# Image 1's loads and weight preparation reordered, image 2's moments and x loads moved, in a two-image attention and motif kernel

## The reference

```
x = x + attention(_gn(x))     # layer 1
x = x + motif(_gn(x))         # layer 2
# attention: qkv = 1x1 conv(x, w_qkv) + b_qkv;  qkv = depthwise 3x3 conv(qkv, w_dw) + b_dw
#   q, k normalised over the pixels; attn = softmax(q k^T * temperature) per head: 4 heads of 24 channels
#   out = 1x1 conv(attn v, w_out) + b_out
# motif: per group of planes the squared distances of shifted patches, the nearest neighbour, then
#   floor(motif * motif_nn * count / Cg), added back over nine shifts
```

## Time and profile before

| | |
|---|---|
| median of 3 runs (lowest, highest) | 1575.14 us (1575.06, 1578.28) |
| profiled execution, its time | 1579.09 us |
| its span | 1577.1 us |
| TensorE, VectorE, ScalarE, GpSimd busy | 85, 73, 56, 43 % of the span |
| mean granted clock of TensorE | 0.934 |
| `prepare` | 0 to 41.2 us |
| attention of image 1, of image 2 begin | 41.2 us, 788.5 us |
| terms of image 1, of image 2 begin | 513.3 us, 1304.5 us |

### The profile page before, as it was taken

How to read it: one execution, slowest core, us unless ns; L and a number is a source line. 1 busy time by engine, 2 the same in 40 slices (tenths; PEclk the granted TensorE clock), 3 DMA queues, 4 the chain that set the end, 5 groups by cost and what they waited for, 6 DMA issues and landing times. The chain is left out here.

```text
span 1577.1 us, 33962 instructions
## 1 busy us (share of the span) xinstructions
PE 1338.1 (85%) x13569; PEld 1079.0 (68%) x13569; DVE 1144.1 (73%) x1903; ACT 879.2 (56%) x950; POOL 680.3 (43%) x680
## 2 busy tenths in 40 slices
PE   0799999996988699999767887889978986999996
PEld 0699887985987355555356777888968983555553
DVE  8577675468864699999645565663786856999995
ACT  1455563212541699999634444542215526999995
POOL 3698892452220335440057566752533303354400
PEclk9999999898999799999969898997989997999998
DMA  6366631792141546453236655423901415464432
GB/s 224 88 209 203 195 90 32 212 273 93 42 168 75 180 123 178 100 142 72 52 101 182 182 155 169 126 62 101 273 5 70 193 62 172 131 178 100 142 72 51
DMA packets 78850, 208.12 MB, mean 132 GB/s; under 512 B 15633, under 2 KB 19827, under 8 KB 76035
## 3 DMA queue, kind: packets, MB, share of 16 engines
q1 hardware_dynamic: 64228, 153.09, 31.5%
q0 software_dynamic: 7296, 40.08, 9.9%
q10 hardware_dynamic: 7168, 12.78, 3.0%
HBM read 89.39 MB, written 67.04 MB: 99 GB/s over the span
## 5 line engine op out<-in xcount | busy, mean ns | idle before, releaser
L1663 PE MATMUL acc<-rnd,ident 128*128 128x376 f32 x1152 | 391.6, 483 | 24.7 <-ACT rnd L1642 24.7
L886 PE MATMUL ps_a<-wa,xa 128*128 128x192 f16 x1536 | 305.3, 251 | 12.7 <-DVE y_s L615 12.5
L1663 PEld LDWEIGHTS acc<-rnd,ident 128*128 128x128 f32 x1152 | 216.5, 192 | 145.3 <-ACT rnd L1642 26.0
L886 PE MATMUL ps_a<-wb,xb 128*128 128x192 f16 x1536 | 303.7, 250 | 0.0
L1510 DVE TENSOR_TENSOR prod<-fc,near 128x1504 f32<-128x1504 f32 x144 | 247.3, 1717 | 33.1 <-DMA near<-f_planes,index 17.4
L1637 ACT ACTIVATE rnd_m<-prod,plus_round,scale 128x1504 f32<-128x1504 f32 x144 | 235.8, 1637 | 61.6 <-DVE prod L1510 51.0
L549 POOL TENSOR_TENSOR vt<-z 96x256 f32<-96x256 f32 x248 | 256.6, 1055 | 18.7 <-ACT z L790 18.6
L1611 DVE SCALAR_TENSOR_TENSOR over<-prod,scale,rnd 128x1504 bf16<-128x1504 f32 x144 | 255.5, 1777 | 0.0
L1555 POOL DMA_INDIRECT near<-f_planes,index x56 | 159.0, 2840 | 209.8 <-DVE prod L1510 201.8
L1642 ACT ACTIVATE rnd<-rnd_m,minus_round 128x1504 f32<-128x1504 f32 x144 | 223.2, 1550 | 4.8
L886 PEld LDWEIGHTS ps_a<-wa,xa 128*128 128x128 f16 x1536 | 154.1, 100 | 19.7 <-issue 18.2
(11 more groups left out here) (304 smaller groups left out, 2390.3 us busy)
## 6 DMA issues: line engine op xcount, KB each, us to landing
xb<-xa ACTq DMA_DIRECT2D x64, 195.0 KB, 2.7
f_planes<-img SPq DMA_DIRECT2D x8, 1536.0 KB, 14.0
fc<-f_planes SPq DMA_DIRECT2D x16, 768.0 KB, 5.5
out<-done_rows POOLq DMA_DIRECT2D x16, 768.0 KB, 8.2
v_a<-xa SPq DMA_DIRECT2D x40, 260.0 KB, 2.7
v_b<-xb SPq DMA_DIRECT2D x40, 260.0 KB, 3.2
xa<-v_a SPq DMA_DIRECT2D x40, 260.0 KB, 4.9
xb<-v_b SPq DMA_DIRECT2D x40, 260.0 KB, 5.5
```

The lines of the kernel that those rows point to most:

```text
L886: mm = lambda a, w, first, end: nc.tensor.matmul(out(i), a, w, start=first, stop=end)
L1663: nc.tensor.matmul(o(m), k["ident"][:, :], rnd[:, n % RNDS, BR * m:BR * m + BR, :], start=False, stop=False, skip_group_check=True)
```

## The change

- `prepare`: SP issues x first. The weights go through ScalarE's queue, w_dw no longer broadcast. TensorE folds: it transposes w_qkv and w_dw (six transposes), ScalarE and GpSimd scale identities into diagonals `diag_w`, and six float32 matmuls w_t x diagonals give the combined weights, which ScalarE rounds to `wqk_hi` and copies to `w_32`, and GpSimd splits to `wqk_lo`. Of the stacking DMAs four stay on SP and nine go to ScalarE's queue (`stack_rest`).
- VectorE in `prepare` has only the statistics and then the moments (`channel_moments`), which were in attention's block.
- VectorE's constants go into units 2 to 9 of image 1 (`constants`), the layout of `wv_u`, `wv_c` to ScalarE in units 4 to 15 (`lay_out`, three activations each, scaled by a column of taps).
- Image 2: its moments are computed at the start of image 1's `motif_terms`, and its x comes in four loads (`load_stretch`, units 0-1, 2-7, 8-19, 20-31).
- Small buffers of `motif_grams` now lie in `g_half`, and `padded` counts in one step more.

```diff
+def channel_moments(nc, dve, c, k, part, mom, mom_c, ps, ps_col, sems):
...
+    group_stats(nc, dve, c, k["stats"], k["dev"], part, ps, mom, sems["stat_ready"], sems["stat_summed"],
+                sems["stat_rooted"])
...
+            for q in range(NQ):
+                sp.dma_start(img[:, QROWS * q:QROWS * (q + 1), :], x[0][:, QROWS * q:QROWS * (q + 1), :]
+                             ).then_inc(x_in[q], 16)
...
+            sp.wait_ge(split, 6)
+            stack_weights(sp, wqk_hi, wqk_lo, k["wa"], k["wb"], stacked)
+            sp.wait_ge(moved, 16 * 18)
...
+            pool.wait_ge(zeroed, COMBINED)
+            nc.gpsimd.tensor_tensor(diag_w[:, 1], k["ident"][0:C, 0:C].unsqueeze(1).to_broadcast([C, 12, C]),
+                                    taps[:, 1, :].unsqueeze(2).to_broadcast([C, 12, C]), ALU.mult).then_inc(zeroed, 1)
...
+            for j in range(6):
+                h, g = divmod(j, 3)
+                at = (slice(None), slice(4 * g, 4 * g + 4), slice(C * h, C * h + C))
+                pool.wait_ge(rounded, j + 1)
+                nc.gpsimd.tensor_tensor(wqk_lo[at], w_32[at], wqk_hi[at], ALU.subtract).then_inc(split, 1)
...
+            channel_moments(nc, dve, c, k, part, mom, mom_c, sums, ps_col, att_sems)
...
+            act.dma_start(w_aug[0:C, :], ins["w_qkv"].rearrange("a b c o -> (a b c) o")).then_inc(weights_in, 16)
...
+            for t in range(12):
+                last = nc.scalar.activation(diag_w[:, 0, t, :], k["ident"][0:C, 0:C], ACT.Identity,
+                                            scale=taps[:, 0, t:t + 1])
...
+                product = ps_w[j][0:CV, 0:BLOCK].rearrange("p (t o) -> p t o", o=C)
+                nc.scalar.activation(wqk_hi[at], product, ACT.Copy)
+                nc.scalar.activation(w_32[at], product, ACT.Copy).then_inc(rounded, 1)
+            act.wait_ge(split, 6)
+            stack_rest(act, wqk_hi, wqk_lo, k["wc"], stacked_c)
...
+                last = nc.tensor.matmul(ps_w[j][0:CV, 0:BLOCK], w_t[:, h, :],
+                                        diag_w[:, h, 4 * g:4 * g + 4, :].rearrange("p t o -> p (t o)"), start=True,
+                                        stop=(g != 1), skip_group_check=True)
...
+    STRETCHES = ((0, 2), (2, 8), (8, 20), (20, UNITS))
...
-            def load_rows(u):
+            def load_stretch(j):
+
                 if b == 0:
                     return
-                if u >= 2:
-                    sp.wait_ge(turned, u)
-                sp.dma_start(img[:, rows_of(u), :], x[b][:, rows_of(u), :]).then_inc(rows_ready[u % 2], 16)
+                if j >= 2:
+                    sp.wait_ge(turned, STRETCHES[j - 2][1] + 1)
+                rows = slice(rows_of(STRETCHES[j][0]).start, rows_of(STRETCHES[j][1] - 1).stop)
+                sp.dma_start(img[:, rows, :], x[b][:, rows, :]).then_inc(rows_ready[j % 2], 16)
 
...
-            for u in range(4):
-                load_rows(u)
+            load_stretch(0)
+            load_stretch(1)
             sp.dma_start(xc[C:XCR].rearrange("p s i x -> p s (i x)"),
                          k["ones_v"][:, :].unsqueeze(1).to_broadcast([6, SLOTS, SLOT])).then_inc(ones_in, 16)
-            sp.wait_ge(padded, 1)
+            sp.wait_ge(padded, 2)
+            load_stretch(2)
             for u in range(AHEAD):
-                load_rows(4 + u)
                 spread(u)
             for u in range(UNITS):
-                if u + 4 + AHEAD < UNITS:
-                    load_rows(u + 4 + AHEAD)
+                if u == 3:
+                    load_stretch(3)
                 if u + AHEAD < UNITS:
                     spread(u + AHEAD)
                 if u < UNITS - SLOTS:
...
+            def constants(u):
+
+                plane_i, plane_f = k["plane_i"], k["plane_f"]
+                if u == 2:
+                    nc.vector.tensor_scalar(k["minus_ident"][:, :], k["ident"][:, :], -1.0, None, ALU.mult)
...
+            def lay_out(t):
+
+                i, d = divmod(t, 3)
+                by = k["taps_v"][:, t:t + 1]
+                for to, of in ((k["wv_u"][:, t, 0:C], slice(0, C)), (k["wv_u"][:, t, C:WV], slice(0, WV - C)),
+                               (k["wv_c"][:, i, 32 * d:32 * d + 32], slice(64, C))):
+                    nc.scalar.activation(to, k["w_v"][:, of], ACT.Identity, scale=by)
...
+                if b == 0 and 4 <= u < 16:
+                    lay_out(u - 4)
...
+            if b + 1 < B:
+                channel_moments(nc, dve, c, k, part, mom, mom_c, next_sums, next_col, att_sems)
...
+                    if i == 0 and b + 1 < B:
+                        channel_moments_sums(nc, pe, k, part, mom_c, next_sums, next_col, att_sems)
+                    if i == 1 and b + 1 < B:
+                        pe.wait_ge(att_sems["mom_col"], 2)
```

More of the change, by code:

```diff
@@ L142, with channel_moments_sums, stack_weights @@
+def channel_moments_sums(nc, pe, k, part, mom_c, ps, ps_col, sems):
+    group_stats_sums(nc, pe, k, part, ps, sems["stat_ready"], sems["stat_summed"])
+    pe.wait_ge(sems["mom_row"], 1)
+    for j in range(2):
+        last = nc.tensor.matmul(ps_col[0:C, j:j + 1], mom_c[0:1, j, :], k["ident"][0:1, 0:1], start=True, stop=True)
+    last.then_inc(sems["mom_col"], 1)
 STACKS, STACKS_C = 4, 9
-def stack_weights(eng, hi, lo, wa, wb, wc, sem, sem_c):
-    def move(dst, src, sem):
+def stack_weights(eng, hi, lo, wa, wb, sem):
+    for dst, src in ((wa[0:C], hi[0:C]), (wb[0:C], lo[0:C]), (wa[C:P], hi[0:32]), (wb[C:P], hi[32:64])):
@@ L205, in _ @@
                              ins["temperature"].rearrange("a h b c -> (a b c) h")[:, h:h + 1]
[L206 to L209, removed]
+                             .to_broadcast([HC, 1])).then_inc(moved, 16)
             sp.wait_ge(lined, 2)
@@ L379, in _ @@
-            last.then_inc(turned, 1)
+            rows = lambda n: k["ident"][0:n, 0:n]
+            for h in range(3):
+                of = w_aug[:, 2 * C:3 * C] if h == 2 else w_qk[:, C * h:C * h + C]
+                nc.tensor.transpose(ps_t[0:C, CV * h:CV * h + CV], of, rows(CV))
+            for h in range(3):
+                of = dw[:, 2 * C:3 * C] if h == 2 else dw_qk[:, C * h:C * h + C]
+                last = nc.tensor.transpose(dw_t[:, h, :], of, rows(KK + 1))
+            last.then_inc(turned, 1)
@@ L628, in _ @@
             for u in range(UNITS):
+                if b == 0:
+                    constants(u)
                 rows_out(2 * u)
@@ L822, in _ @@
                 norm(u)
+            act.wait_ge(padded, 2)
             for u in range(AHEAD):
@@ L869, in rows_in @@
                 if b > 0:
-                    pe.wait_ge(rows_ready[u % 2], 16 * (u // 2 + 1))
+                    j = sum(u >= end for _, end in STRETCHES)
+                    pe.wait_ge(rows_ready[j % 2], 16 * (j // 2 + 1))
             def turn(u):
@@ L922, in _ @@
             turn(0)
-            group_stats_sums(nc, pe, k, part, ps_s, stat_ready, stat_summed)
-            pe.wait_ge(mom_row, 1)
-            for j in range(2):
-                last = nc.tensor.matmul(ps[0][0:C, 0, j:j + 1], mom_c[0:1, j, :], k["ident"][0:1, 0:1], start=True,
-                                        stop=True)
-            last.then_inc(mom_col, 1)
             nc.tensor.matmul(ps_g[0:C, 0:2 * C2], k["zeros"][:, 0:C], k["zeros"][:, 0:2 * C2], start=True,
@@ L1004, in _ @@
                     pe.wait_ge(pivot_in, 1)
-                    nc.tensor.matmul(ps_s[:, 0, :], k["mean_ones"][:, :], part[:, 0, :], start=True, stop=True
+                    nc.tensor.matmul(ps_s[:, 0, :], k["mean_ones"][:, :], part[:, :], start=True, stop=True
                                      ).then_inc(pivot_out, 1)
```

371 lines of the change are left out of this document (189 added, 182 removed).

## The result

The changed kernel takes 1520.5 us (median of 4 runs, 1516.9 to 1526.5) where the kernel before took 1575.1 beside it: a ratio of 0.9665, 95% interval 0.9616 to 0.9713. In a second set it took 1517.7 (6 runs, 1509.7 to 1526.0), ratio 0.962 (0.9581 to 0.9658). It is faster, by 54.6 and 57.7 us, where 68 were forecast: 10.7 to 13.5 us are missing. The profiled execution took 1516.9 us, its span is 1514.8.

The account below looks back on a forecast made before the run. TensorE waiting for late x rows in image 2 (41.9 us) and uncovered starts of both images were the bounds; terms -46.7 - 11.4 + 0.2 - 4.2 - 7.3 + 1.7 = -67.7 gave 1511.4, by run median 1507 us; range 1500 to 1521.

Parts of the forecast that it names:

- Four loads: Image 2's convolution stretch: x in four loads removes the 12 waits for img, stretch as in image 1; -46.7 us.
- bounds are nothing and 6 us, I take 1: Image 2, fourth load ahead of spread(6) in SP's queue: delay to the spread priced at 1 us.
- the slack: Image 2's spreads: each is issued about two units before its use, which should hide queue delay.
- Start of image 2: Block start to first convolution: moments leave it, z earlier, then image 1's pace of 9.7 us; -11.4 us, bounds -4 to -12.
- units 2 to 5 no longer wait: Start of image 2: these units no longer wait for single loads, so image 1's 9.7 us from z to convolution holds.
- the wait moves to the spreads: Rival, image 2: spread(0) and spread(6) each come a full 6 us late, +11, 1518 us; chance 0.12.
- one queue: Reason for the spreads rival: the large loads and the spreads are in the same SP queue.
- Start of image 1: Preparation and attention's start: x issued first, block end at 37.0 (-4.2 us), then z sooner after the block's start (-7.3 us).
- W: Start of image 1: time the weights land, estimated 5 to 10, taken as 7.6; block end at W + 29.4.
- W = 19, the strict reading: Start of image 1: weights wait for all of x on the shared DMA engines; block ends at 48.4.
- Moments in the ramp: Start of image 1's terms: image 2's moments fit VectorE's 8.23 us wait for the first gather; +0.2 us, at most 1.
- Additions in the units: Image 1's units: constants on VectorE add 1.5 us and lay_out on ScalarE 0.2; +1.7 us, bounds 0 and 13.

Follow-up runs that it names:

- load 3 behind: Changed kernel with image 2's load 3 (2.4 MB) issued behind the first three spreads instead of ahead of them; 1511.9 us, single run.
- weights first: Changed kernel with loads 2 to 4 of image 1's x held on SP until the five weight loads have landed; 1507.0 us, single run.
- stacking split: Changed kernel with three of the nine stacking DMAs moved from ScalarE's queue behind SP's four; 1521.6 us, single run.

## Why the prediction was wrong, and where it was right

The direction and the mechanism were right, the size was not: the sum was 67.7 us, the same terms measured 56.6. Of the 11.1 between them, 5.1 are in the term of the four loads and 5.0 in the start of image 2. Most of both comes from one step that failed: what a large load does to the spreads issued behind it was priced at 1 us and at nothing, and TensorE waited 8.2 us for it.

- **Four loads, -46.7: right mechanism, one term too small.** The 12 pauses went and the stretch became image 1's, up to the wait at unit 6. The step that failed is "bounds are nothing and 6 us, I take 1": it measured 4.8, 3.9 and 4.8 us of wait (the change twice, load 3 behind). Two numbers in it were off. I gave 2.3 MB 6 us, from x alone at 430 GB/s; it took 12.4, in which the 16 engines were 99% busy and moved twice its bytes (317 GB/s times 14.4 us is 4.6 MB, half of it x, the rest saves, duplicates and spreads). And the slack was not two units: the spread is issued 8.3 to 3.9 us before its use, with a unit of some 6.2 us.
- **Start of image 2: forecast -11.4, measured -6.4.** `z` came as forecast (5.6 us after the block's start, forecast 5.3). Then image 1's 9.7 us became 14.3. Load 3 passed not in 7 us but in 10.7, and the first spread needed 8.2 us from issue to use where image 1 needs 4.9: 3.3. Most of the rest, 1.6, comes from "units 2 to 5 no longer wait": ScalarE takes one `z` of rows in load 2 ahead of its first `xa`, and TensorE waited 1.4 for that load.
- So the rival **"the wait moves to the spreads"**, 0.12, is what happened, nearly at its price: 8.2 of 11 us. My reason against it, the slack, was the false step. My reason for it, one queue, was not the cause either: with the loads on GpSimd's queue the waits are 8.2 us as well.
- **Start of image 1.** W was 10.1, not 7.6, through x in flight (2.3 us, weights first). Half of this term was lost, 2.0 us. Some 1.5 of it is this chain, since attention starts at 37.5 once the root no longer stands behind it (stacking split); the other 0.5 is the statistics' chain, which begins at 7.5 and not at 6.9. The weights' sum held in total: `split` full at W + 17.2 (18.4 forecast), block at W + 28.9 (29.4). In part that is luck: GpSimd's own work was shorter than forecast (`diag_w` 2.1 us for 3.0), but it stood 3.1 us for TensorE's folds and ScalarE's evacuations, which were meant to run under it. W = 19, the strict reading, did not come. The piece from the block to the first convolution held to 0.1.
- **Moments in the ramp, +0.2:** right, -0.1.
- **Additions in the units, +1.7:** +1.1 between two profiles, +0.9 between the means of nine and of two. The laying out was not tried by itself, and how much of this is the constants stays open.
- **Not forecast:** -6.2 in the rest of image 1's attention and grams. That differs from execution to execution and is not the change (below). Without it the terms give -56.6, and 1575.1 - 56.6 = 1518.5, between the two medians.

## What to carry to other kernels

A large transfer can hold up small ones issued while it is under way, whichever queue carries either (8.2 us here on one queue and on two); so cost it by what else the engines move at that time, not by its speed alone, and compare it with the time from the small transfer's last issue to its use, read from the timeline. Cut a prefetch into pieces that pass within that slack, and issue each behind the urgent transfers and still ahead of its own use: both sides have a price here (4.8 us too large, 6.0 us too late). When two chains end a block within 3 us of each other, shortening one gives at most their distance.

## What the runs showed of the hardware

The spread between runs of one kernel goes mostly with TensorE's granted clock. Ten runs of the changed kernel lie between 1509.7 us at 0.954 and 1526.5 at 0.941: some 1.3 us for each 0.001. It shows in a stage that the change does not touch, from the softmax of image 1 to its grams; before, then after, then in the kernel with loads on GpSimd:

```profile
265.30:378.30 113.00, 97.07 (x1884) 93.22 (x1882) 68.18 (x264) 22.23 (x50) 44.60 (x62) 0.91 0.62 188
```

```profile
256.81:365.89 109.08, 90.29 (x1880) 86.79 (x1878) 68.17 (x264) 22.21 (x51) 44.54 (x62) 0.96 0.66 194
```

```profile
257.32:361.94 104.62, 90.03 (x1882) 86.91 (x1880) 68.21 (x264) 22.22 (x51) 44.58 (x62) 0.97 0.64 203
```

VectorE's busy time is the same to 0.04 us in all three. TensorE's is 97.1 us at a clock of 0.91 and 90.3 and 90.0 at 0.96 and 0.97. All 14 profiles fall into these two groups: seven at 0.90 to 0.91, TensorE 96.8 to 97.1 us busy, the stage 110.8 to 113.0; and seven at 0.95 to 0.97, 89.7 to 91.9 us busy, 104.6 to 110.3. The kernel before is in the first group, and so is the changed kernel in its second profile (112.8), so the change did not make the difference. The clock is not all of it: the last two lines above are 4.5 us apart at nearly the same busy time, and 4.0 of it is TensorE standing idle with no wait that the profile shows (6.2 and 2.2 us). Effects of 1 to 3 us, as in the block of preparation, can only be read from the marks of a stage, not from the runs' times, and the marks scatter by 1 to 3 us too: 205.0 to 208.3 for one and the same stretch in nine profiles. What sets the clock of one execution stays open.
